# Low k of the second half of the pixels: written into its stack by VectorE, or brought there by a transfer

## The reference

```
q = Wq x + bq        # 32 x 1024 per image
k = Wk x + bk        # 32 x 1024
v = Wv x + bv        # 256 x 1024
scores[i, j] = sum over 32 channels of q[:, i] * k[:, j]
attn = softmax of scores over j
out[c, i] = sum over j of v[c, j] * attn[i, j]   + x[c, i]
```

## Time and profile before

| what | us |
|---|---|
| median of 3 runs | 174.59 |
| lowest, highest | 173.0, 174.74 |
| the profiled execution's own time | 174.27 |
| its span, first to last instruction | 172.4 |
| TensorE busy in it | 163.1 |
| VectorE busy in it | 138.4 |
| ScalarE busy in it | 107.9 |
| GpSimd busy in it | 42.3 |

### The profile page before, as it was taken

The page is one execution under the profiler, slowest core; times in us unless marked ns, Lnnn a source line. Parts: engine busy times, 40 slices in busy tenths (PEclk is TensorE's granted clock), DMA queues, the critical chain, the costliest instruction groups (busy, mean ns, idle before and its releaser), DMA issues. The chain is left out here.

```text
span 172.4 us, 2481 instructions
## 1 busy us (share of the span) xinstructions
PE 163.1 (95%) x814; PEld 129.1 (75%) x814; DVE 138.4 (80%) x220; ACT 107.9 (63%) x195; POOL 42.3 (25%) x51
## 2 busy tenths in 40 slices
PE   7778999996999999999999999999999999999992
PEld 5356978773888897776888898785888897886781
DVE  0679899799899989799899988799874889876353
ACT  3556896784884765676984764764784765655310
POOL 6279730043222030133221030033121020002500
PEclk9999999999999999999999999999999999999998
DMA  5933257063400330063400330062400330003003
GB/s 191 322 110 91 64 229 243 0 143 89 169 2 0 91 122 0 0 150 82 167 0 4 91 124 2 2 152 77 171 0 0 93 118 8 0 0 122 0 2 122
DMA packets 7502, 14.45 MB, mean 84 GB/s; under 512 B 1281, under 2 KB 1793, under 8 KB 7489
## 3 DMA queue, kind: packets, MB, share of 16 engines
q1 hardware_dynamic: 6656, 13.37, 24.0%
q0 software_dynamic: 416, 0.79, 2.0%
q10 hardware_dynamic: 416, 0.13, 0.3%
HBM read 4.59 MB, written 4.19 MB: 51 GB/s over the span
## 5 line engine op out<-in xcount | busy, mean ns | idle before, releaser
L765 PE MATMUL acc<-w_hi,v_hi 128*128 128x512 f32 x128 | 51.8, 404 | 0.1
L765 PE MATMUL acc<-w_hi,v_lo 128*128 128x512 f32 x128 | 50.5, 394 | 0.0
L411 ACT ACTIVATE w_full<-st 128x512 f32<-128x512 f32 x64 | 37.5, 595 | 20.6 <-PE st L751 20.6
L315 POOL TENSOR_TENSOR w_lo<-w_full,w_hi 128x512 fp32r<-128x512 f32 x16 | 21.8, 1365 | 80.0 <-ACT w_full L411 61.1
L380 ACT ACTIVATE dump<-slot,negmax 128x1024 f32<-128x1024 f32 x29 | 32.4, 1118 | 14.1 <-DVE negmax L521 13.8
L773 PE MATMUL acc<-w_lo,v_hi 128*128 128x512 f32 x120 | 38.4, 396 | 0.0
L564 DVE TENSOR_TENSOR w_lo<-w_full,w_hi 128x512 fp32r<-128x512 f32 x48 | 34.1, 711 | 5.0 <-issue 0.5
L521 DVE TENSOR_REDUCE negmax<-slot 128x1 f32<-128x1024 f32 x29 | 35.3, 1218 | 2.3 <-PE slot L688 2.3
L765 PEld LDWEIGHTS acc<-w_hi,v_hi 128*128 128x128 f32 x128 | 24.1, 188 | 7.4 <-issue 1.4
L555 DVE CAST w_hi<-w_full 128x512 fp32r<-128x512 f32 x51 | 21.6, 424 | 8.8 <-ACT w_full L411 7.9
L765 PEld LDWEIGHTS acc<-w_hi,v_lo 128*128 128x128 f32 x128 | 24.2, 189 | 5.0
(11 more groups left out here) (81 smaller groups left out, 175.9 us busy)
## 6 DMA issues: line engine op xcount, KB each, us to landing
out<-o_sb SPq DMA_DIRECT2D x7, 512.0 KB, 2.9
x_sb<-x SPq DMA_DIRECT2D x3, 1024.0 KB, 6.1
k_b<-k_a SPq DMA_DIRECT2D x8, 192.0 KB, 2.5
q_b<-q_a SPq DMA_DIRECT2D x8, 192.0 KB, 2.6
k_a<-qk_parts SPq DMA_DIRECT2D x12, 64.0 KB, 1.9
q_a<-qk_parts SPq DMA_DIRECT2D x12, 64.0 KB, 2.3
x_sb<-x SPq DMA_DIRECT2D x1, 512.0 KB, 3.5
x_sb<-x SPq DMA_DIRECT2D x2, 256.0 KB, 5.2
```

The lines of the kernel that those rows point to most:

```text
L315: nc.gpsimd.tensor_tensor(w_lo[:, r, :], w_full[:, r, :], w_hi[:, r, :].bitcast(fp32), ALU.subtract).then_inc(w_split_pool, 1)
L411: nc.scalar.activation(w_full[:, r, :], st[:, j % 2, :], ACT.Exp).then_inc(exp_done, 1)
L765: nc.tensor.matmul(acc[:, c, :], v[:, j, ch], w_hi[:, r, :], start=(j == 0 and v is v_hi), stop=False)
```

## The change

The low k of the second half of the pixels (h = 1) is no longer brought from qk_parts to k_a by a transfer. For h = 1 `add_rest` writes the low q only, and a second tensor_tensor of VectorE, right behind it, adds the k partitions and writes them straight to k_a[32:64]. It counts k_lo_put, for which TensorE waits before the scores, and SP before the copy to k_b. It waits first for the scores of the image before, which read k_a. The half h = 0 stays as it was.

```diff
                 for h in range(2):
                     sp.wait_ge(qk_split, 2 * (b - 1) + h + 1)
-                    blocks(sp, k_a, 1, 2, h, ka_in[h])
+                    if h == 0:
+                        blocks(sp, k_a, 1, 2, h, ka_in[h])
                     blocks(sp, q_a, 2, 3, h, qa_in[h])
...
-                sp.wait_ge(ka_in[1], 2 * DMA * (b + 1))
+                sp.wait_ge(ka_in[1], DMA * (b + 1))
+                sp.wait_ge(k_lo_put, 2 + b + 1)
                 sp.wait_ge(k_dup_in[1], DMA * (b + 1))
                 second_stack(k_b, k_a, 1, kb_in[1])
...
             def add_rest(b, h):
                 dve.wait_ge(qk_rested, 2 * (b - 1) + h + 1)
-                nc.vector.tensor_tensor(qk_parts[2 * CQK:P, cols(h)], qk_home(b, h)[2 * CQK:P, :],
-                                        qk_rest[2 * CQK:P, cols(h)], ALU.add).then_inc(qk_split, 1)
+                k_lo, q_lo = slice(2 * CQK, 3 * CQK), slice(3 * CQK, P)
+                rows = q_lo if h == 1 else slice(2 * CQK, P)
+                nc.vector.tensor_tensor(qk_parts[rows, cols(h)], qk_home(b, h)[rows, :],
+                                        qk_rest[rows, cols(h)], ALU.add).then_inc(qk_split, 1)
+                if h == 1:
+
+                    dve.wait_ge(scores_ready, JT * b)
+                    nc.vector.tensor_tensor(k_a[CQK:2 * CQK, cols(1)], qk_home(b, 1)[k_lo, :],
+                                            qk_rest[k_lo, cols(1)], ALU.add).then_inc(k_lo_put, 1)
...
                 if t == 0:
                     pe.wait_ge(qa_in[0], 2 * DMA * b)
                     pe.wait_ge(q_dup_in[0], DMA * b)
+                    pe.wait_ge(k_lo_put, 2 + b)
                     for h in range(2):
-                        pe.wait_ge(ka_in[h], 2 * DMA * b)
+                        pe.wait_ge(ka_in[h], (2 - h) * DMA * b)
                         pe.wait_ge(k_dup_in[h], DMA * b)
```

## The result

The changed kernel takes 178.34 us in the median of four runs (177.59 to 179.24), the kernel before 173.81 in four runs beside it (173.0 to 174.74). The ratio is 1.0252, with a 95% interval of 1.0199 to 1.0306: slower, by 4.5 us between the medians. The profiled execution of the changed kernel is the longest of its four, 179.24 us with a span of 177.4; the one before took 174.27 with 172.4, so the two spans differ by 5.0.

What follows compares the result with a forecast made beforehand. VectorE's chain up to `finish`, which releases TensorE's L765, was taken as the bound, so removing the transfer gains nothing. Images 1 to 3 add 0.37 + 1.70 + 1.83 = 3.90 us to 174.27: 178.2 us, range 175.8 to 179.0.

Steps and rivals of the forecast that it cites:

- What bounds: Before L765: VectorE's chain up to `finish` (L574) releases TensorE, at a constant 0.86 to 0.87 us; the scores' start hardly matters.
- Rivals B and C: B: removed transfer was the bound, 172.4, chance 0.06; C: image 1's return balances images 2 and 3, 174.3, 0.06.
- The operation: New 32x512 tensor_tensor behind `add_rest(b, 1)` on VectorE: 0.72 us per image, between 0.61 and 0.78.
- the L574 rows: Profile rows of `finish`, claimed to take its usual 1.41 us a pair beside a running L315, so the new operation passes too.
- Image 1: Cast of tile 8 blocked by L315 instead of the subtraction; `finish` at 42.07 instead of 41.70, +0.37 us.
- the subtraction, 0.09 later: Image 1, tile 8: subtraction starts 0.09 us after the blocked cast ends at 41.25, running 41.34 to 42.03.
- Image 2: Subtraction of tile 8 shifts to 80.31, inside L315, and ends at 81.98 instead of 80.28; `finish` +1.70 us.
- Image 3: L315 passes ahead of the cast of tile 8, which ends at 120.35; `finish` at 121.17 instead of 119.34, +1.83 us.
- The sum: Three images together: 0.37 + 1.70 + 1.83 = 3.90 us, carried to the end.
- The starting point: The profiled execution of the kernel before, 174.27 us, to which 3.90 was added for 178.17.
- Rival A: Shift alone, L315 meets nothing new: +1.8 to +2.9 us, so 176.1 to 177.2; chance 0.23.
- Rival D: Chain late a second time after `finish`: new operation held by L315 or longer pause, 0.44 to 0.8 more, 178.7 to 179.2; chance 0.05.

Runs made afterwards that it cites:

- the operation alone: Kernel before plus the new 32x512 operation written to an unread spare tile, old transfer kept; 178.43 us, ratio 1.0197 to the kernel before.
- the transfer alone: Kernel before without the low-k transfer for h = 1 in images 1 to 3, nothing in its place; 175.19 us, ratio 1.0047.
- the six repeated runs: The changed kernel once more, unaltered, for more runs and a second trace; 178.87 us, ratio 1.0249 to the kernel before.
- the quarter operation: Changed kernel with the new operation over 128 of the 512 columns; 175.54 us, ratio 1.0070 to the kernel before.
- GpSimd's wait: GpSimd starts its low part of tile 9 only after VectorE's subtraction of tile 8; changed kernel 174.82 us (1.0056), kernel before 174.22 us (0.9970).
- the memsets: Four one-column memsets at VectorE's start, with GpSimd's wait: changed kernel 174.31 us; kernel before, also with 12 filler matmuls, 172.42 us.

## Why the prediction was right

Forecast 178.2, range 175.8 to 179.0, measured 178.34.

- **What bounds.** That `finish` releases L765, read from the distance of 0.86 to 0.87, held in all of the traces where the landing did not come later, that of the kernel without the transfer among them. Shown by the operation alone (same distances with the transfer kept) and by the transfer alone (nothing gained). Rivals B and C fell with it.
- **The operation.** Forecast 0.69 + 0.03, measured 0.69 in all three images with the next start at 0.72. That it passes beside L315's counterpart was forecast from the L574 rows, and it did: L317 took 1.26 beside it. For this I named and the earlier trace rows; only the earlier trace rows show it, as in the earlier trace rows L315 ends at 41.12, before L574 starts at 41.70. The Trainium skill, SBUF — State Buffer, section "Who interferes with whom", says that a VectorE instruction with at most one SBUF input outside the two-port modes does not contend with GpSimd. This agrees with the trace (0.69 beside a running L317).
- **Image 1.** Forecast +0.37, measured +0.75. The blocked cast was as forecast (0.93 against 0.96 foreseen). The step that failed is "the subtraction, 0.09 later": it came 0.50 later, for the pause.
- **Image 2.** Forecast +1.70, measured +1.69.
- **Image 3.** Forecast +1.83 with L315 ahead of the cast. Measured +1.69 with L317 behind the cast, as in image 2, since the stretch in front was 0.43 shorter. The step that failed is that I took VectorE's lateness against GpSimd in the earlier trace rows as a property of the third image. It came from the pause of 0.46 at 104.96, which was in the trace before and which I did not follow; it went when the instructions shifted. Over the twelve traces the stretch from `finish` of image 2 to the second `add_rest` of image 3 is 35.90 to 35.93 us in the four that have the pause there and 35.41 to 35.57 in the other eight. Net 1.69 − 0.43 = +1.26.
- **The sum.** 0.75 + 1.69 + 1.26 = 3.70 against 3.90: two misses of 0.4 to 0.6 with opposite signs. That the total is so near is luck in this part; the 1.69 of image 2 is not.
- **The clock.** Not in the sum at all; I wrote nothing on it. With 1.51 us it makes up most of what the two spans differ by beyond the 3.70. Nine of the ten runs of the changed kernel have a granted clock of 0.986 to 0.990, of before only about half. Inside the two groups the difference is near the forecast: 178.87, the median of the six repeated runs, against 175.17, the median of the 15 runs of before at the lower clock, is 3.7; the one run of the changed kernel at 0.997, 177.59, against 173.5, the median of the other 14 of before, is 4.1. More runs with the fall bring the medians 4.5 apart, 4.3 in the repetition.
- **The starting point.** I added 3.90 to 174.27, one execution without the fall. It was among the longer ones of its group, whose median is 173.5. From there the sum gives 177.4, near the one run of the changed kernel without the fall. That the forecast also meets the median of runs that nearly all have the fall is luck: a starting point 0.8 too high stands in for part of the clock's 1.5.
- **Rival A, the length alone**, is excluded by the quarter operation and by GpSimd's wait: of the cost in images 2 and 3, 0.72 is length and 0.97 the meeting.
- **Rival D, more than I count.** Its sum does not come out: 0.44 to 0.8 on top of 178.17 is 178.6 to 179.0, not 178.7 to 179.2. The repeated runs, 178.87, lie in it by their number, but not for its reasons: the new operation was not held by L317 and did not pause at its wait. What came on top was a pause at another instruction and the clock.

## What to carry to other kernels

A wait for a transfer that the profile names may be worth nothing: look at the next instruction of the same engine that has to stop, and whether its distance to another engine's operation is the same in every repetition. If an operation is put into a chain, ask not only for its length but which engine it now meets behind it; here 0.72 us of work pushed a subtraction behind GpSimd's and became 1.69, and one wait on the idle engine took 0.97 of that away. Where the runs of a kernel fall into two groups by granted clock, a few filler matmuls in its longest TensorE wait are a cheap trial.

## What the runs showed that I had not expected

- TensorE's clock fell to half speed behind the wait of the first image in both traces of the changed kernel, in which TensorE's matmuls stood idle for 0.40 and then 1.94 us. The traced execution of the kernel before, with 1.64 us idle in one piece, did not have the fall; that about half of its runs had it is read from their granted clock of 0.986 to 0.990 and from the traces of its two variants with that clock, which show the fall at that place. The fall took 1.51 us of time, and filler matmuls in the wait made it stay away in all 36 runs that had them. What decides from run to run stays open: the traced execution of the quarter operation kept its clock behind 2.38 us of idle matmuls, while that of the kernel before with GpSimd's wait lost it behind 1.64.
- VectorE makes a pause of 0.46 to 0.51 us in front of a subtraction, which no wait and no other engine explains. It stands at the 64th or the 192nd of VectorE's records in eleven of the twelve traces, and four tiny instructions at the start moved it. The five traces of the kernel before and its variants have one more, of 0.44, in front of the subtraction that is the 320th record; the profile names TensorE for it, but with the memsets it stands one subtraction earlier (163.34 instead of 166.46), so it is likely of the same kind. What makes these pauses was not measured.
- Blocking between GpSimd and VectorE is decided by who comes first: 0.22 us earlier and GpSimd takes 1.62, 0.18 us later and VectorE takes 1.66. The one that comes second ends a fixed time behind the end of the first, which is a little less than its own usual length: 0.54 to 0.55 for the subtraction (0.69 alone), 0.28 to 0.30 for the cast (0.43), 1.15 for GpSimd (1.28). So meeting costs nearly the whole rest of the other's operation; the two do not run side by side.
